# Attention with an expert layer on one core: the first exponential of a tile waits for its scores alone, and a head's maxima are joined behind the next head's first maximum

## The reference

```
q, k, v = xn @ Wq.T + bq, xn @ Wk.T + bk, xn @ Wv.T + bv     # per batch and head: 2048 x 16
scores  = (q * 16**-0.5) @ k.T                               # 2048 x 2048
probs   = softmax(scores, axis=-1)
att     = (probs @ v) @ Wo.T + bo
x + att + expert_layer(xn)
```

## Time and profile before

| | us |
|---|---|
| median of 3 runs | 3170.62 |
| profiled execution | 3171.86 |
| its span on the core | 3170.1 |
| TensorE matmuls busy | 3119.6 (98%) |
| VectorE busy | 2876.4 (91%) |
| ScalarE busy | 2476.4 (78%) |
| GpSimd busy | 947.7 (30%) |

### The profile page before, as it was taken

One profiled execution on the slowest core, in us unless ns is written; L12 is line 12 of the kernel. 1 busy time (PEld: TensorE's weight loads), 2 busy tenths in 40 slices (PEclk: granted clock), 3 DMA queues, 4 the chain that ended last, 5 costly groups with the idle time before them and its releaser, 6 DMA issues.

```text
span 3170.1 us, 74308 instructions
## 1 busy us (share of the span) xinstructions
PE 3119.6 (98%) x23912; PEld 1565.3 (49%) x23912; DVE 2876.4 (91%) x4046; ACT 2476.4 (78%) x4631; POOL 947.7 (30%) x1403
## 2 busy tenths in 40 slices
PE   7999999999999999999999999999999999999998
PEld 6544444444444444444444444444444444688887
DVE  7758999999999999999999999999999999466666
ACT  3557888888888888888888888888888888544443
POOL 2551222222222222222222222222222232344444
PEclk9999999999999999999999999999999999999999
DMA  5684333333333333333333333333333331455554
GB/s 197 198 239 92 58 58 58 58 58 63 61 62 59 65 61 65 58 58 58 58 58 58 58 58 58 60 63 61 65 62 61 61 74 35 139 163 162 160 162 126
DMA packets 139865, 272.00 MB, mean 86 GB/s; under 512 B 30144, under 2 KB 75264, under 8 KB 127296
## 3 DMA queue, kind: packets, MB, share of 16 engines
q1 hardware_dynamic: 137472, 266.71, 39.8%
q10 hardware_dynamic: 2112, 1.35, 0.2%
HBM read 173.59 MB, written 84.93 MB: 82 GB/s over the span
## 4 chain that ended last, share of the span: by engine, by line
PE 89%; issue 1%; DVE 1%; POOL 0%; DMA 0%; SPq 0%; ACT 0%; POOLq 0%; DVEq 0%; ACTq 0%
PE a_ps L919 35%; PE s_ps L909 35%; PE m_ps L901 9%; PE o_ps L1188 5%; PE h_ps L1178 5%; PE inv_ps L1211 1%; POOL g_lo L1412 0%; DMA mask_bc<-mask_b 0%; PE inv_ps L1198 0%; PE o_ps L1219 0%; DVE bn_z L1306 0%; DVE z L1301 0%; DVE g L1292 0%; ACT num_hi L1270 0%; SPq L1095 0%
## 5 line engine op out<-in xcount | busy, mean ns | idle before, releaser
L985 DVE TENSOR_REDUCE half_max<-m_ps 128x1 f32<-128x1024 f32 x3009 | 2377.0, 858 | 30.7 <-PE m_ps L901 13.8
L869 ACT ACTIVATE prob<-s_ps 128x512 f32<-128x512 f32 x4096 | 2155.1, 602 | 292.4 <-PE s_ps L909 289.9
L909 PE MATMUL s_ps<-q_feat,k_feat 50*128 50x512 f32 x4096 | 1472.9, 451 | 2.4 <-ACTq L859 2.4
L901 PE MATMUL m_ps<-k_feat,q_feat 48*128 48x512 f32 x4012 | 1336.5, 433 | 0.2 <-DVE half_max L985 0.2
L919 PE MATMUL a_ps<-prob,v_head 128*32 128x512 f32 x12280 | 1202.1, 463 | 4.8 <-issue 4.8
L909 PEld LDWEIGHTS s_ps<-q_feat,k_feat 50*128 50x128 f32 x4096 | 683.1, 184 | 931.4 <-ACT prob L869 852.9
L901 PEld LDWEIGHTS m_ps<-k_feat,q_feat 48*128 48x128 f32 x4012 | 650.1, 185 | 8.4 <-DVE half_max L985 1.0
L919 PEld LDWEIGHTS a_ps<-prob,v_head 128*32 128x32 f32 x12280 | 242.9, 108 | 474.7 <-issue 455.7
L704 POOL COPY v_head<-v_all 128x256 f32 (+1 forms) x64 | 25.3, 397 | 838.9 <-PE a_ps L919 838.9
L1259 ACT ACTIVATE g_hi<-g 128x512 fp32r<-128x512 f32 x128 | 81.0, 632 | 214.1 <-DVE g L1292 173.7
L711 POOL CAST shift<-row_max 128x16 fp32r<-128x16 f32 x63 | 12.3, 195 | 776.0 <-DVE row_max L987 776.0
(11 more groups left out here) (145 smaller groups left out, 2007.3 us busy)
## 6 DMA issues: line engine op xcount, KB each, us to landing
q_feat<-q_parts SPq DMA_DIRECT2D x384, 128.0 KB, 4.2
k_feat<-k_parts SPq DMA_DIRECT2D x384, 128.0 KB, 5.7
q_parts<-parts SPq DMA_DIRECT2D x32, 512.0 KB, 4.3
k_parts<-parts SPq DMA_DIRECT2D x32, 512.0 KB, 4.3
att_dram<-att SPq DMA_DIRECT2D x64, 256.0 KB, 6.3
mask_bc<-mask_b SPq DMA_DIRECT2D x128, 128.0 KB, 4.4
x_in<-in_x SPq DMA_DIRECT2D x16, 512.0 KB, 4.4
xn_dram<-xn SPq DMA_DIRECT2D x16, 512.0 KB, 5.1
```

The source lines that it names most:

```text
L869: act.activation(prob[tile(r, kt) % R][:, cols(j)], s_ps[slot(r, kt, j) % R][:, :], ACT.Exp).then_inc(exped, 1)
L901: pe.matmul(m_ps[j // 2][:, (j % 2) * BLK:(j % 2 + 1) * BLK], q_feat[r % 2][LOW, qt * P:(qt + 1) * P], k_feat[r % 2][LOW, j * BLK:(j + 1) ...
L909: pe.matmul(s_ps[slot(r, kt, j) % R][:, :], k_feat[r % 2][UP, kt * P:(kt + 1) * P], q_feat[r % 2][UP, cols(j)], start=True, stop=True).the ...
L985: dve.tensor_reduce(half_max[r][:, qt, o:o + 1], max_source(m_ps, o), AX.X, ALU.max).then_inc(maxed, 1)
```

## The change

The exponential's wait for `weighed` is removed; the waits for `parts_stored`, which stand once, at the second tile of head 0, stay. The join of a head's maxima is moved: it was at the end of `maxima(n)`; now it stands in `maxima(n + 1)`, between the first query tile's 1024-wide reduction and its first 512-wide one. The join of the last head stays behind its last reduction.

```diff
             def exp(g, r, kt, j, first=False):
-                if j == 0:
-                    act.wait_ge(weighed, tile(g, kt) + 1)
-                    if first and kt == 1:
-                        for done in parts_stored:
-                            act.wait_ge(done, 16 * NBLK + 16)
+                if first and (kt, j) == (1, 0):
+                    for done in parts_stored:
+                        act.wait_ge(done, 16 * NBLK + 16)
                 act.wait_ge(scored, slot(g, kt, j) + 1)
...
+            def join_maxima(n):
+                dve.wait_ge(maxed, n * OPS + OPS + 3)
+                dve.tensor_reduce(row_max[n % R][:, :], half_max[n % R][:, :, :], AX.X, ALU.max, negate=True).then_inc(row_maxed, 1)
+
             def maxima(n, r, turn_at=TURN_AT, lo=0):
                 for qt in range(lo, ST):
                     last_key = 0
                     for o, banks in enumerate(MAX_BANKS):
+                        if (qt, o) == (0, 1) and n > 1:
+                            join_maxima(n - 1)
                         if (qt, o) == (turn_at, 1):
                             turn_shift(n - 1)
...
-                dve.wait_ge(maxed, n * OPS + OPS + 3)
-                dve.tensor_reduce(row_max[r][:, :], half_max[r][:, :, :], AX.X, ALU.max, negate=True).then_inc(row_maxed, 1)
-
             maxima(1, 1, turn_at=None, lo=EARLY)
             for n in range(2, HEADS):
                 maxima(n, n % R)
+            join_maxima(HEADS - 1)
             turn_shift(HEADS - 1)
```

## The result

The changed kernel takes 3134.3 us, median of 4 runs (3133.5 to 3135.8), against 3170.8 of the kernel before in the same comparison: ratio 0.9883, 95% interval 0.9871 to 0.9896, so 36.5 us less. The forecast was 3138 and 32.7 us less, in a range of 3126 to 3157.

What follows compares the result with a forecast made beforehand. The prediction took the loop S3, E3, E4, S7, next S3 to set the 4.80 us pair. 504 x 0.06 = 30.2 us plus 62 x 0.04 = 2.5 for the join made 32.7, so 3138 us, range 3126 to 3157.

Steps and rivals of the forecast that it cites:

- The pair: Two key tiles' work in the attention loop, eight score matmuls, 4.80 us; forecast to fall to 4.74.
- E4: First exponential of a pair's odd tile, on ScalarE; forecast to gain 0.06 us per pair, 30.2 us in all.
- E0: First exponential of a pair, on ScalarE; starts 0.06 us earlier without its wait, claimed to buy nothing on the path.
- C: Rival at the exponentials: S4's arrival delays E4, a second wait is free; at most 2.5 us gained, 3168 to 3171; chance 0.04.
- S4: Score matmul on TensorE whose exponential is E4; recorded to end early, but claimed to come late, behind M5.
- M5: Maxima matmul on TensorE, ahead of S4 in program order; E4 forecast to start 0.07 us after its end, not 0.14.
- E3: Exponential just ahead of E4 on ScalarE; E3 to E4 forecast to fall from 0.57 us to 0.49 to 0.51.
- B: Rival at E4: it starts at ScalarE's own rate, 0.08 us sooner; 42.8 us gained, 3128; chance 0.10.
- Rival A: VectorE takes the wait's place, only half of the 0.06 us per pair is had; 17.6 us gained, 3153; chance 0.08.
- GpSimd's reserve of 3.8 us: Time forecast to remain between GpSimd's finished split shift and the transpose needing it, after the join's result comes 1.1 us later.
- D: Rival: the later join delays transpose, shift rows and next head's first score; slower, 3200 at 1 us late; chance 0.03.

## Why the prediction was right, and what it missed

- The pair. Forecast 0.06 us at E4 and nothing at E0; the median pair, taken at each position within a head but the boundary's, fell from 4.793 to 4.733, and the two waits put back one by one gave 30 us and nothing. 504 x 0.06 = 30.2 us stands. C is refuted by the idle wait on E4, which cost the same 30 us though it waited for nothing.
- The cause. That S4 is seen behind M5 had been argued from one distance; with M5 moved, E3 to E4 fell to 0.49 in the kernel before without a wait being touched, and S4's semaphore came 0.23 us sooner after S4's end. B was wrong by M5, as the prediction said, and what it would have brought is had by moving M5 as well (3127.7 and 3126.1 us against B's 3128). What the prediction read from the page is weaker: the 853 us of idle loads that end with an exponential are not where the gain was, as the page above shows; the pair that it followed was the right place.
- The join. Forecast 0.12 of VectorE, measured 0.11; the boundary pair is 4.73 like the others, so 62 x 0.05 = 2.9 us against the 2.5 of the sum. That VectorE's lateness of 0.16 with the old place would cost 0.10 was right too (0.12). What the prediction's split hides is that only the two together give its sum: the exponentials alone gained 27 us and not 30, and the join is 7 to 9 of the 36 in the shorter pairs, and not 2.5.
- Rival A did not come, and the moved join has its part in that: with the join in its old place VectorE takes back 7.4 us, half of the 15 that A would have cost.
- GpSimd's reserve of 3.8 us was as forecast, and D did not come.
- The last head's pairs stayed at 4.71.

The forecast is 3.8 us short, and 32.7 lies just outside the interval (33 to 41 us). The join gave 0.4 more than the sum had. Besides, the kernel before had 8 pairs, 25 pairs apart, in which E4 came 0.28 us late. Two rows of one of them, E3 and E4:

```profile
1567.97 0.60 ACT L869 ACTIVATE prob<-s_ps 128x512 f32<-128x512 f32 x1 [0.21 <-PE s_ps L909]
1568.83 0.60 ACT L869 ACTIVATE prob<-s_ps 128x512 f32<-128x512 f32 x1 [0.26 <-issue]
```

None of them is left in the changed kernel's first profile, which is 8 x 0.28 = 2.2 us that the sum lacked; the three other kernels with a second wait on E4 and the old order of M5 have 4, 5 and 8 such E4, those without it 0 to 2. It stands as "issue", so nothing of the profile was waited for. The kernel with only the join moved has its eight at the same pairs, and in the kernel before a transfer of the instruction queue q14 starts 0.6 to 2.2 us after each of these E4, while such transfers are some 30 us apart on average. That queue's packets are 82 with the 1024 waiting instructions of ScalarE and 74 without, so the late E4 seem to lie where code for ScalarE is being loaded; that the loading is what delays them is not shown. Where TensorE leaves its loop over heads, two pairs took 15.2 us before and 12.8 after; in the changed kernel's second profile they took 11.2, but the first three pairs took 20.3 in place of 16.3. These places differ by 2 to 4 us between profiles of one program, so the 2.4 us between the first two profiles cannot be put down to the change, and the cause stays open.

## What to carry to other kernels

In this kernel a second wait on an instruction cost time only where what the instruction needs arrived last. Look for the one instruction in the loop whose releaser arrives late and whose end somebody waits for, and count nothing for the others. A redundant wait there can be taken out or hidden by an issue order that lets the awaited result arrive a little earlier. When a bound engine's period shrinks, price the stalls of the next engine again: what cost 0.04 us a head before cost 0.12 after.

## What the runs showed of the hardware

- A score's completion was reported only behind that of a matmul issued ahead of it in other rows of the array, though the score is recorded to start and end first: S4's semaphore rose 245 ns after S4's recorded end, and 14 ns after it once M5 was issued behind S4. In nine of ten of the 504 pairs E4 started 130 to 132 ns behind M5's end with two waits and 71 to 72 with one. The Trainium skill ("TensorE: Matmul & The Clock Gate", Part 3: Packing small matmuls, the mechanism) has ends in program order, and this agrees with it; its order of starts is not what the records show.
- Five waits already met per pair on ScalarE cost nothing that could be measured behind running exponentials (starts 0.48 us apart with and without); one met wait on E4 cost 0.06 us.
- On VectorE the join with a wait for the reduction just issued started 0.71 us after it, where the next reduction starts 0.59 to 0.60 after: 0.12 us. The Trainium skill ("VectorE: DVE Perf Modes", the DRAIN you can't avoid) says that a semaphore in a chain of copies cost nothing extra; here the join's hold on VectorE fell from 0.24 to 0.11 us when that wait was met beforehand.
